# Local attention and a ternary projection on eight cores: blocks of 488 queries, scores by query rows, DMA transposes

## The reference

```python
q, k, v = xn @ w_q + b_q, xn @ w_k + b_k, xn @ w_v + b_v     # 16 heads of 64
scores  = q . k over the 7 tokens s-3 .. s+3, times 1/8       # -inf outside 0..S-1
out     = softmax(scores) @ v_window, then @ w_o + b_o
w_tern  = clip(round(wf / scale), -1, 1), scale = max(mean(|wf|), 1e-5)
result  = x + out + xn @ (w_tern * scale).T
```

## Time and profile before

| what | value |
|---|---|
| three runs, median (lowest to highest) | 949.66 us (949.29 to 949.71) |
| the profiled execution: span of its slowest core | 949.3 us |
| spans of the eight cores | 941.7 to 949.3 us |
| mean granted TensorE clock of the cores | 0.988 to 0.992 |
| busy share: PE, PEld, DVE, ACT, POOL | 82%, 60%, 34%, 38%, 10% |
| first projection of the loop (PE L475) starts at | 156.8 us |
| one step of the loop | 22.54 us |
| transfers of HBM: read, written | 58.89 MB, 16.78 MB |

### The profile page before, as it was taken

The page is one execution under the profiler, slowest core; times in us unless marked ns, Lnnn a source line. Parts: engine busy times, 40 slices in busy tenths (PEclk is TensorE's granted clock), DMA queues, the critical chain, the costliest instruction groups (busy, mean ns, idle before and its releaser), DMA issues.

```text
span 949.3 us, 21922 instructions; the slowest of 8 cores (941.7 to 949.3 us)
## 1 busy us (share of the span) xinstructions
PE 781.6 (82%) x8386; PEld 571.7 (60%) x8386; DVE 324.7 (34%) x566; ACT 363.6 (38%) x537; POOL 98.9 (10%) x72
## 2 busy tenths in 40 slices
PE   0000027899999999999999999999999999999984
PEld 0000014677777777777777777777777777777652
DVE  3112374223333333333333333333333333333221
ACT  0232113444444444444444444444444444444320
POOL 0000000001111111111111111111111111111112
PEclk9999999999999999999999999999999999999997
DMA  0479751101111111112211111111111111111211
GB/s 28 116 241 310 256 179 49 54 28 53 68 67 69 68 66 66 67 69 77 75 68 67 68 66 68 68 67 68 68 67 68 68 67 66 58 46 48 66 47 33
DMA packets 20531, 77.07 MB, mean 81 GB/s; under 512 B 1855, under 2 KB 1991, under 8 KB 20430
## 3 DMA queue, kind: packets, MB, share of 16 engines
q1 hardware_dynamic: 15582, 58.89, 17.4%
q0 software_dynamic: 4848, 16.78, 6.0%
HBM read 58.89 MB, written 16.78 MB: 80 GB/s over the span
## 4 chain that ended last, share of the span: by engine, by line
PE 80%; DMA 11%; DVE 4%; issue 2%; ACT 2%; DVEq 1%; POOL 0%; SPq 0%; ACTq 0%; POOLq 0%
PE p_qk L475 25%; PE p_of L727 13%; PE p_qk L692 13%; PE p_qk L638 13%; PE p_sc L748 5%; PE p_sc L590 3%; DMA xl<-x 3%; DMA wstage<-wq 2%; PE p_of L721 2%; PE p_qk L488 2%; DMA wstage<-wf 2%; PE p_qk L754 2%; PE p_tx L427 1%; DMA wstage<-wk 1%; DMA wstage<-wv 1%
## 5 line engine op out<-in xcount | busy, mean ns | idle before, releaser
L799 POOL TENSOR_TENSOR osb<-osb,ffn_sb 122x1024 f32<-122x1024 f32 (+1 forms) x34 | 80.1, 2355 | 822.8 <-DVE osb L793 803.5
L475 PE MATMUL p_qk<-xnt,wq_b 128*128 128x122 bf16 (+1 forms) x2176 | 128.2, 217 | 1.2 <-DVE xnt L441 1.2
L692 PE MATMUL p_qk<-wfT_b,xnt 128*122 128x512 bf16 (+1 forms) x544 | 123.6, 380 | 5.4 <-ACT v_sb L651 1.9
L727 PE MATMUL p_of<-wo_b,atT 128*122 128x512 bf16 (+1 forms) x544 | 126.7, 387 | 0.0
L638 PE MATMUL p_qk<-wv_b,xnt 128*128 128x512 bf16 (+1 forms) x544 | 124.6, 383 | 0.1
L475 PEld LDWEIGHTS p_qk<-xnt,wq_b 128*128 128x128 bf16 x2176 | 118.5, 98 | 9.0 <-issue 9.0
L475 PE MATMUL p_qk<-xnt,wk_b 128*128 128x122 bf16 (+1 forms) x2176 | 121.3, 215 | 0.4 <-ACT qme L522 0.4
L522 ACT CAST qme<-p_qk 64x488 bf16<-64x488 f32 (+1 forms) x86 | 39.2, 478 | 213.0 <-PE p_qk L488 205.8
L475 PEld LDWEIGHTS p_qk<-xnt,wk_b 128*128 128x128 bf16 x2176 | 115.7, 97 | 7.7 <-issue 7.6
L614 DVE TENSOR_TENSOR au_buf<-e_buf,mk_sb 128x976 bf16<-128x976 bf16 (+1 forms) x68 | 47.1, 693 | 207.4 <-ACT e_buf L603 207.4
L727 PEld LDWEIGHTS p_of<-wo_b,atT 128*122 128x122 bf16 (+1 forms) x544 | 70.5, 134 | 54.3 <-issue 16.0
(11 more groups left out here) (77 smaller groups left out, 737.7 us busy)
## 6 DMA issues: line engine op xcount, KB each, us to landing
xl<-x SPq DMA_DIRECT2D x33, 488.0 KB
xr<-x SPq DMA_DIRECT2D x33, 488.0 KB
out<-osb POOLq DMA_DIRECT2D x33, 488.0 KB, 7.2
wstage<-wf SPq DMA_DIRECT2D x8, 1024.0 KB, 6.2
wstage<-wq SPq DMA_DIRECT2D x8, 512.0 KB, 11.6
wstage<-wk SPq DMA_DIRECT2D x8, 512.0 KB, 6.1
wstage<-wv SPq DMA_DIRECT2D x8, 512.0 KB, 5.6
wstage<-wo SPq DMA_DIRECT2D x8, 512.0 KB, 5.7
```

Source lines behind the costliest of these rows:

```text
L475: f = (lambda pp, m2, k2, c2, r2, wb2, st2, sp2: (lambda e: e.matmul(p_qk[0:128, c2:c2 + psz_of(pp)], wb2[0:128, k2 * H + 128 * m2: k2 * H ...
L692: f = (lambda ii, k2, j2, q2: (lambda e: e.matmul(p_qk[0:tsz_of(ii), 512 * j2:512 * j2 + 512], xnt_ap()[:, k2, q2:q2 + tsz_of(ii)], wfT_b[ ...
L727: f = (lambda ii, k2, j2, a2: (lambda e: e.matmul(p_of[0:tsz_of(ii), 512 * j2:512 * j2 + 512], atT[:, :].rearrange("p (s c n) -> p s c n", ...
L799: inc("gpsimd", "g", (lambda ii, s2, o2: (lambda e: e.tensor_add(osb[0:tsz_of(ii), o2 * H:(o2 + 1) * H], osb[0:tsz_of(ii), o2 * H:(o2 + 1) ...
```

## The change

The kernel is written anew on the same split of the tokens. The main differences:

- **Projections by block.** q and k are projected for a block of 4 tiles at once: 8 matmuls with 488 (q) or 512 (k) columns for each of 8 groups of 128 output columns, a quarter of a block in each step (`qk_part`). Each group is a job with a PSUM bank of its own out of two (`next_bank`); a job waits until the job two places earlier has been copied out. Biases are added in the copies.
- **Scores by query rows.** A head's scores have its 122 queries as rows and 128 keys as columns; heads of 64 channels are read from the upper or lower half of one buffer. DVE adds a mask of 0 or -1e30 (L296 of the new kernel) and takes the row maximum (L303); ACT exponentiates head by head, with that maximum as its bias and the row sum as a second output (L311, 8 in a half, 16 in a step); DVE takes reciprocals and multiplies (L318, L322).
- **Transposes by DMA.** The normed tile and both halves of the weights are transposed by transfers of 128 x 1024 bf16 that SP issues (L190, L331), three in a step. PE transposes nothing.
- **Values stationary.** The weighted sum has v standing in the array (64 columns) and 122 queries moving, so that its output is already transposed for the output projection; no denominators are computed on PE.
- **One PSUM tile.** The ternary product and the output projection accumulate into one tile `p_f`; DVE adds it to `xr`, to which POOL has added the bias row.
- **Layer norm** by `bn_stats` on DVE, eight tiles ahead; ACT does only its Ln and Exp of one column.
- **Loads and stores.** x for the norm is loaded as 128 rows; the residual load and the store have 122 rows, and the store is issued by SP. Weights are loaded and cast by 16 transfers that POOL issues at the start; wf comes transposed from the host.
- **Before the loop** eight tiles are normed, q and k of the first two blocks projected, and the first tile's weights made.

```diff
@@ the jobs of projection @@
+        def next_bank():
+            n = jobs[0]
+            jobs[0] += 1
+            if n >= 2:
+                q.need("tensor", ("pev", n - 2))
+            return n, p_p[:, 512 * (n % 2):512 * (n % 2) + 512]
+        def q_job(b, c):
...
+            q.need("tensor", ("w", "wq"), *[("xnt", BW * b + w) for w in range(nw)])
+            for k in range(8):
+                q.do("tensor", lambda e, k=k: e.matmul(
+                    bank[:, 0:TQ * nw],
+                    w_b["wq"][:, k * H + 128 * c:k * H + 128 * c + 128],
...
+            q.need("scalar", ("pj", n), "bq8")
...
+            q.do("scalar", lambda e: e.activation(
+                qt[b % 2][:, c * BW * TQ:c * BW * TQ + TQ * nw], bank[:, 0:TQ * nw], AF.Identity,
+                bias=bq8[:, c:c + 1], scale=0.125), ("pev", n))
@@ softmax @@
+        def mask_max(i, hf):
...
+            q.do("vector", lambda e: e.tensor_tensor(
+                heads(sm[hf]), heads(p_s),
+                mk[0:TQ, KW * mt:KW * mt + KW][:, None, :].broadcast_to([TQ, 8, KW]),
+                ALU.add), ("sadd", i, hf))
...
+            q.do("vector", lambda e: e.tensor_reduce(
+                nmx[hf][0:TQ, :], heads(sm[hf]), AX.X, ALU.max, negate=True), ("nmx", i, hf))
+        def exps(i, hf):
...
+            for h in range(8):
+                q.do("scalar", lambda e, h=h: e.activation(
+                    sm[hf][0:TQ, KW * h:KW * h + KW], sm[hf][0:TQ, KW * h:KW * h + KW], AF.Exp,
+                    bias=nmx[hf][0:TQ, h:h + 1], accum_out=den[hf][0:TQ, h:h + 1]),
+                    ("exp", i, hf) if h == 7 else None)
+        def e_transpose(i, hf):
+            k = 2 * (i % 2) + hf
+            q.need("sync", ("en", i, hf))
+            if i >= 2:
+                q.need("sync", ("av", i - 2))
+            q.dma("sync", f"te{k}", lambda e: e.dma_start_transpose(
+                et[k][:, :].rearrange("p (h n) -> p h n", h=8, n=KW), en[hf][:, :]), ("et", i, hf))
@@ residual and store @@
+        def xr_load(i):
+            n = own_rows(i)
+            if i >= NR:
+                q.need("sync", ("st", i - NR))
...
+        def store(i):
+            n = own_rows(i)
+            q.need("sync", ("out", i))
+            q.dma("sync", f"o{i % NR}", lambda e: e.dma_start(
+                out_h[TQ * i:TQ * i + n, :], xr[i % NR][0:n, :]), ("st", i))
@@ the loop @@
-        for s in range(NP + 3):
...
+        for s in range(NW):
+            b, w = divmod(s, BW)
+            n = s + 1
+            if s + 2 < NW:
+                xr_load(s + 2)
+            if n < NW:
+                xr_bias(n)
+            if s >= 1:
+                out_add(s - 1)
+                store(s - 1)
+            if s + AHEAD < NW:
+                layer_norm(s + AHEAD)
+            if b + 1 < NB:
+                if b >= 1:
+                    qk_part(b + 1, w)
+            if n < NW:
+                scores(n, 0)
+                mask_max(n, 0)
+            if s + AHEAD < NW:
+                normalise(s + AHEAD)
+                xn_transpose(s + AHEAD)
+                if s + AHEAD + NX < NW:
+                    x_load(s + AHEAD + NX)
+            if n < NW:
+                exps(n, 0)
+                v_job(n, 0)
+                v_job(n, 1)
+                v_evict(n, 0)
+                v_evict(n, 1)
+                scores(n, 1)
+                mask_max(n, 1)
+                weights(n, 0)
+                e_transpose(n, 0)
+            att_v(s)
+            att_evict(s)
+            f_proj(s)
+            if n < NW:
+                exps(n, 1)
+                weights(n, 1)
+                e_transpose(n, 1)
+            o_proj(s)
```

More of the change, by code:

```diff
@@ L1 @@
+import contextlib
 import numpy as np
-import ml_dtypes
 import concourse.bass as bass
@@ L15 @@
 NC = 8
[L16 to L20, removed]
-OWN = 4096
[L23 to L45, removed]
+OWN = 4096
+TQ = 122
+KW = 128
+NW = 34
@@ new lines, with nwin, own_rows, __init__ @@
+BW = 4
+NB = (NW + BW - 1) // BW
+ROWS = TQ * (NW - 1) + KW
+NEG = -1.0e30
+def nwin(b):
+    return min(BW, NW - BW * b)
+def own_rows(i):
+    return min(TQ, OWN - TQ * i)
+class Queues:
+    def __init__(self):
+        self.items = {e: [] for e in ("sync", "gpsimd", "tensor", "vector", "scalar")}
+        self.count = {}
+        self.point = {}
+        self.seen = {e: {} for e in self.items}
+    def do(self, eng, f, key=None):
+        sem = None
+        if key is not None:
+            sem = eng
+            self.count[sem] = self.count.get(sem, 0) + 1
+            self.point[key] = (sem, self.count[sem])
+        self.items[eng].append((f, sem, 1))
+    def dma(self, eng, slot, f, key):
+        self.count[slot] = self.count.get(slot, 0) + 16
+        self.point[key] = (slot, self.count[slot])
+        self.items[eng].append((f, slot, 16))
+    def need(self, eng, *keys):
+        for key in keys:
+            sem, value = self.point[key]
+            if self.seen[eng].get(sem, 0) < value:
+                self.seen[eng][sem] = value
+                self.items[eng].append((None, sem, value))
@@ L64, in build_program @@
[L64 to L76, removed]
-        last_wait[eng] = {}
-        prog[eng].append(("inc", f, sem, n))
@@ L914, in _ @@
         @block.scalar
[L915 to L933 removed]
+        def _(e):
+            run(e, q.items["scalar"])
@@ L934, in make_masks @@
+    return nc
+def make_masks(core):
+    t = np.arange(128)[:, None]
+    j = np.arange(KW)[None, :]
+    band = (j >= t) & (j <= t + 6)
+    m = np.stack([band, band, band])
+    half = NC // 2
+    if core % half == 0:
+        m[0][:, :3] = False
     if core % half == half - 1:
-        m2[tszl + 3:, :] = 0.0
-    m[2] = m2
-    return m.astype(ml_dtypes.bfloat16)
+        m[2][:, OWN + 3 - TQ * (NW - 1):] = False
+    add = np.where(m, np.float32(0.0), np.float32(NEG)).astype(np.float32)
+    return np.ascontiguousarray(add.transpose(1, 0, 2).reshape(128, 3 * KW))
```

1196 lines of the change are left out of this document (376 added, 820 removed).

## The result

The changed kernel takes 1001.52 us (median of 4 runs, 996.77 to 1009.46) against 949.68 us before (4 runs, 949.29 to 951.07): ratio 1.055, interval 1.050 to 1.060. It is slower; the forecast was 936 us. The profiled execution took 996.77 us, its span 995.2 us. In one execution each of e4, e5, e7 and e10 further down, the highest in its brackets, some cores ran at a lower granted clock; the medians count it, which moves them by less than 1 us, and the ratios leave it out.

What follows compares the result with a forecast made beforehand. The prediction took a dependence chain plus a clock fall, 25.0 us a step, to bound the loop. 145 us ahead, 63 for three steps, 550 for 22, 129 for six, 17 and 32 made 936 us; range 865 to 1060.

Steps and rivals of the forecast that it cites:

- the pair: The two DMA engines on which the prediction put the 122-row load and store, plus a share of each transposition.
- PE's work: Loop step: PE's matmuls sum to 18.9 us against 22.5 before, so PE does not stay the bound.
- The chain: Loop step: dependences through exponentials, copies, layer norm, q and k jobs, scores and maxima take 22.4 us at full clock.
- The clock: Loop step: PE's wait of about 2.9 us before the second q job drops its clock, adding 2.6 us: 25.0 us.
- D: Loop step: time the two loaded DMA engines need for load, store, x and three transposes, 24.5 us, hidden under 25.0.
- the transposes are dear: Rival, 20%: transposes on the two loaded engines set the step from 1.37 us each; 1034 us total at 2.5 us each.
- The transpositions' price: Loop step: each 262 KB transpose costs 1.2 us on each DMA engine, taken from packets of 256 B.
- The far dearer transposition: Loop step: by a skill page, eight blocks one after another give 10.5 us a transfer, 31 us a step, near 1150 us total.
- The store on SP at 9.6 us: Loop step: the 122-row store issued by SP is priced like the 122-row loads, 488 KB at 52 GB/s, 9.6 us.
- Ahead of the loop: Start of kernel: casting transfers at 304 GB/s, then projections, ternary pieces and bias row; first loop scores at about 145 us.
- The first steps: Loop start: three steps without projections at 21 us each, between the chain without them (18) and D; 63 us.
- The likeliest case: Whole kernel: the forecast itself, from 905 to 965 us, 46%: 29 faster, 4 the same, 13 slower.

Runs made afterwards that it cites:

- e4: Changed kernel with the edits of e2 and e3 together (both transfers cut, wv and wo held back): 812.02 us, ratio 0.854 to the kernel before.
- e5: Changed kernel with only the residual load cut into 112 and 10 rows, the store left whole on SP: 842.79 us, ratio 0.885 to the kernel before.
- e7: e4 with the layer norm's Ln and Exp issued behind the copies of q on ACT: 770.31 us, ratio 0.810 to the kernel before.
- e10: e7 with the first pass over wf beside block 0's projections and the ternary pieces beside block 1's: 772.89 us, ratio 0.814.
- e3: Changed kernel with the loads of wv and wo held back until the eighth transposed tile has landed: 976.59 us, ratio 1.029 to the kernel before.
- e12: e2 with one more ACT copy of 1024 columns between the layer norm and the first copy of q: 883.80 us, ratio 0.930.
- e8: Changed kernel with the store put behind the transposition of xn and the load of x in SP's queue: 999.65 us, ratio 1.051.
- e6: Changed kernel with only the store cut into 112 and 10 rows, the residual load left whole: 864.37 us, ratio 0.909 to the kernel before.
- e11: Changed kernel with a fourth transposition a step, into a tile that nobody reads: 1048.17 us, ratio 1.104 to the kernel before.
- e2: Changed kernel with residual load and store each cut into 112 and 10 rows, both on SP: 833.62 us, ratio 0.878 to the kernel before.
- e1: Changed kernel with the store of 122 rows issued by POOL instead of SP: 870.57 us, ratio 0.917 to the kernel before.
- e9: Kernel before the change with both its loads of 122 rows (xl and xr) cut into 112 and 10 rows: 932.43 us, ratio 0.982.

## Why the prediction was wrong

The sum was 936 us of span and came out at 995.2: 35 us too little ahead of the loop, 8 in the first three steps, 21 in the 22 steps, 4.5 too much in the rest. Two steps of it failed, one ahead of the loop, where the transpositions beside the casting transfers were given no time of their own, and one in the loop, where the load on the pair was compared with a chain that was too long. The first alone turns the sign: 936 us and the 22 that e3 gives back there are 958, against 949.7. By its own steps:

**PE's work: right.** 18.9 us forecast, 18.98 measured in a step.

**The chain: its shape right, its size too long.** Its order is what ACT's and PE's timelines show, and e7 (the link cut, 1.9 us gone) and e12 (a link added, 0.98 us more) show that it sets the step where nothing else does. It is 20.88 us, not 22.4: the exponentials are cheaper. On ACT in the changed kernel:

```profile
564.74 0.38 ACT L311 ACTIVATE sm<-sm,nmx 122x128 f32<-122x128 f32 x1
565.03 0.18 ACT L311 ACTIVATION_READ_ACCUMULATOR sm<-sm,nmx 122x1 f32 x1
565.13 0.38 ACT L311 ACTIVATE sm<-sm,nmx 122x128 f32<-122x128 f32 x1
```

A pair takes 0.39 us, so both overlaps are there; eight are 3.1 us, not 3.8, and twice 0.7 is 1.4 of the 1.5 us. (The forecast's lower end of 0.40 us was itself added up wrongly: 0.40 and 0.20 less 0.11 twice is 0.38.)

**The clock: wrong for this kernel.** The wait before the second q job is 1.7 us, not 2.9, and behind it the clock stays at 1.00. The 2.6 us that the forecast added for the fall are not there. The one in the earlier trace rows came after 2.9 us; e12 shows falls after 2.7 us. None was seen after 1.7. Between these it is open: the two jobs behind a wait of 2.22 us in e3 took 5.16 us, those behind 2.56 us in e8 3.49, at full clock. Where the changed kernel does lose clock is behind the long waits for the transposed tile (0.55 from 588.18 to 591.50 us); what that costs beside the load on the pair was not tried.

**D at 24.5 us, "just hidden under 25.0": this is the step that failed in the loop.** The forecast had the two engines at D = 24.5 us and the chain with its fall at 25.0, and let the chain win. D was nearly right: from 298.14 to 800.79 us there are five blocks, 25.1 us a step (and the same in e3, whose loop is that of the changed kernel). But it had 20.88 us to hide under. So the loaded engines set the pace, in one long wait at the first q job of a block and shorter ones for the weights. The step came out near 25 us for the other reason, and that the forecast's time for the loop was close was luck, two errors that met: a chain too long by 1.5 us with a fall of the clock that wasn't there, 2.6 us, gave nearly the time of the pair. It was the rival "the transposes are dear" in all but the price: it named this wait, at this job, but had it decide from 1.37 us a transposition on, because it set D against 25.0. Against 20.88 it decides as soon as both slow transfers are there (9.6 + 9.6 + 1.7 = 20.9) and the transpositions come on top, at any price. e5 and e6 (either transfer cut: steps of 20.88 us from tile 5 to 26), e8 (order: no effect) and e11 (1.5 us for one transposition more) show each part. The traces give the busy share of the 16 engines together and not of single ones, so that it is two of them that are full is inferred from these runs. The transpositions' price was 1.2 us forecast; e11 puts it at 1.5 us over the run (with which D is 25.4 us) and at 1.7 over four blocks (26.9 against 25.2 us a step). The far dearer transposition of the prediction's estimate, 10.5 us for eight blocks one after another, is not there: in e2 each lands 3.0 to 3.1 us after its issue.

**The store on SP at 9.6 us: right.** In e5, where it alone is whole, the DMA moves mostly 47 to 62 GB/s for some 9.5 us behind the cut load, with a tenth of the engines. e1 and e6 take it off the pair and the loop falls to 20.88 us.

**Ahead of the loop: the largest miss, and the step that failed there.** The forecast let the casting transfers go at 304 GB/s and had q and k of block 0 start at 46 us and end at 72; they start at 71.56 and end at 106.94, and all of the 35 us is there by then: block 1's end (151.7 against 116) and the loop's start are late by the same. The transfers were indeed slower, 190 GB/s over the first 75 us, but that didn't set the start: wk, issued up to 6.7 us, has landed by 41 us, and the first q job waits for the transposed tile. The sum has nothing for the transpositions there, and each of three stood 11 to 15 us. e3 shows 22 us of the 35. In e3 the first q job starts at 47.20 us, 1.2 us later than forecast, and q and k end at 83.72. Those 36.5 us are 16 jobs of 1.7 us (the forecast had 15 and 26 us), a wait of 3.52 us for ACT's first copy of q, and some 5.8 us that the first four jobs lose at low clock: eight matmuls with 488 columns take 3.41 us in them and 1.84 later, and the granted clock of the second pair is 0.52. ACT's copy stands behind the layer norm's operations of the eighth tile, at 55.61 us.

**The first steps.** Forecast 21 us each, they are 14.7 us on average when both transfers are cut, and 23.7 with them whole: the backlog on the pair again, at its largest because three residual loads are issued together (the transposition behind them holds SP for 19.71 us).

**The chances.** The likeliest case was forecast with 46%, dear transposes with 20%. The time lies inside the range, but the forecast itself was 1.4% faster than before and the kernel is 5.5% slower: that side had 45%.

## What to carry to other kernels

Before a transfer is put in a queue, look at its row count: 122 rows ran on about two engines and 112 + 10 on most of 16, and that was worth 168 of 1001 us here. A transfer that is slow but hidden becomes dear when something urgent, here a transposition (in e2 over 90% of 16 engines are busy for 1.2 us with one), must pass behind it. Add up the load of the busiest engines for a step and compare it with the step after the change, computed with its lower bound, not with the value that one expects. And a chain of small waits that happens to be longest should be checked with each of its doubtful terms at its cheapest, since the next limit shows itself only then. Ahead of a loop, too, transfers that run beside each other must be priced together: three transpositions beside casting transfers made the start 22 us late.

## What was not expected of the hardware

- A store of 122 rows went on two engines from SP (47 to 62 GB/s and a tenth of 16 engines, e5) and on many from POOL (0.28 MB in 1.5 us, 58% of 16 engines, e1).
- A transposition of 262 KB held SP 1.24 us when alone, 11 to 15 us while casting transfers of POOL ran, and in the changed kernel up to 18.10 us behind a load and a store of 122 rows and 19.71 us behind three such loads.
- PE's clock was 1.00 over steps with waits of 1.7 us (e2), and in 17 of 21 steps it fell after waits of 2.7 us, at a cost of 1.66 us of the following 3.5 us of work (e12).
- Cutting two loads at the start of the kernel before brought its first projection forward by 18.6 us (e9).
